# Attention scores of a perceiver block: 12 block-diagonal matmuls become 48 matmuls on 32x32 pieces of the array

## The reference

```python
q = (query @ Wq).reshape(B, L, H, D).transpose(0, 2, 1, 3)   # B=128, L=32, H=16, D=32
k = (key @ Wk).reshape(B, S, H, D).transpose(0, 2, 1, 3)     # S=257
v = (value @ Wv).reshape(B, S, H, D).transpose(0, 2, 1, 3)
attn = jnp.einsum('bhld,bhsd->bhls', q * SCALE, k)
attn = jax.nn.softmax(attn, axis=-1)
x = jnp.einsum('bhls,bhsd->bhld', attn, v)
x = x.transpose(0, 2, 1, 3).reshape(B, L, C)
return x @ Wo + bo
```

## Time and profile before

| | |
|---|---|
| median of 3 runs | 2917.51 us (2917.2 to 2921.46) |
| profiled execution, its span (the page gives no other time of it) | 2917.1 us |
| cross-attention within the span | about 126 to 1912 us |
| mean granted TensorE clock over the span | 0.980 |

### The profile page before, as it was taken

How to read it: one execution, slowest core, us unless ns; L and a number is a source line. 1 busy time by engine, 2 the same in 40 slices (tenths; PEclk the granted TensorE clock), 3 DMA queues, 4 the chain that set the end, 5 groups by cost and what they waited for, 6 DMA issues and landing times. The chain is left out here.

```text
span 2917.1 us, 54809 instructions
## 1 busy us (share of the span) xinstructions
PE 2794.1 (96%) x18492; PEld 1704.0 (58%) x18492; DVE 1668.3 (57%) x3620; ACT 1267.4 (43%) x2954; POOL 776.4 (27%) x1530
## 2 busy tenths in 40 slices
PE   7999999999999999999999999957999999899999
PEld 4455555555555555555555555534666666566666
DVE  7555555555555555555555555556665666656664
ACT  4344444444444444444444444423433443344444
POOL 2233333333333333333333333211111111111110
PEclk9999999999999999999999999978999999999999
DMA  4211111111111111111111111022000000000000
GB/s 143 83 56 55 62 41 40 40 48 41 40 40 48 41 40 40 48 41 40 40 48 41 40 40 48 13 84 66 15 30 15 15 14 22 22 14 14 14 23 15
DMA packets 65959, 118.49 MB, mean 41 GB/s; under 512 B 12016, under 2 KB 32496, under 8 KB 65392
## 3 DMA queue, kind: packets, MB, share of 16 engines
q1 hardware_dynamic: 65904, 117.76, 12.4%
HBM read 109.06 MB, written 8.65 MB: 40 GB/s over the span
## 5 line engine op out<-in xcount | busy, mean ns | idle before, releaser
L656 DVE SCALAR_TENSOR_TENSOR kT_lo<-psum,kT_hi 128x512 f16<-128x512 f32 x256 | 177.1, 692 | 440.2 <-ACT kT_hi L587 440.2
L591 ACT ACTIVATE v_hi<-psum 128x512 f16<-128x512 f32 x256 | 152.8, 597 | 552.7 <-PE psum L746 552.7
L746 PE MATMUL psum<-c_hi,xWk_hi 128*128 128x512 f16 x1024 | 388.1, 379 | 2.3 <-PEq L136 2.3
L746 PE MATMUL psum<-xWv_hi,c_hi 128*128 128x512 f16 x1024 | 388.3, 379 | 0.0
L746 PE MATMUL psum<-xWv_lo,c_hi 128*128 128x512 f16 x1024 | 388.1, 379 | 0.0
L746 PE MATMUL psum<-xWv_hi,c_lo 128*128 128x512 f16 x1024 | 388.1, 379 | 0.0
L746 PE MATMUL psum<-c_lo,xWk_hi 128*128 128x512 f16 x1024 | 388.1, 379 | 0.0
L746 PE MATMUL psum<-c_hi,xWk_lo 128*128 128x512 f16 x1024 | 388.1, 379 | 0.0
L118 POOL TENSOR_TENSOR c_lo<-ctx_raw,c_hi 128x1024 f16<-128x1024 f32 x128 | 272.5, 2129 | 429.8 <-ACT c_hi L583 419.2
L662 DVE SCALAR_TENSOR_TENSOR v_lo<-psum,v_hi 128x512 f16<-128x512 f32 x256 | 177.1, 692 | 360.4 <-ACT v_hi L591 360.4
L597 ACT ACTIVATE e<-psum,neg_max 128x257 f32<-128x257 f32 x512 | 236.3, 474 | 281.9 <-DVE neg_max L651 281.9
(11 more groups left out here) (195 smaller groups left out, 5986.9 us busy)
## 6 DMA issues: line engine op xcount, KB each, us to landing
ctx_raw<-in_ctx_main SPq DMA_DIRECT2D x128, 512.0 KB, 3.3
xs<-in_x SPq DMA_DIRECT2D x8, 1024.0 KB, 5.5
v_rep<-v_last_rows SPq DMA_DIRECT2D x512, 16.0 KB, 2.3
xb<-in_x SPq DMA_DIRECT2D x16, 512.0 KB, 3.3
out<-res_out SPq DMA_DIRECT2D x32, 256.0 KB, 2.0
ffn_raw<-in_w_t SPq DMA_DIRECT2D x11, 512.0 KB, 3.4
late_raw<-in_late_w SPq DMA_DIRECT2D x4, 1024.0 KB, 4.7
res<-in_w_t SPq DMA_DIRECT2D x5, 512.0 KB, 3.5
```

Source lines behind the costliest of these rows:

```text
L591: nc.scalar.mul(v_hi[u][:, t, :], v_bank(t), W_UNSCALE).then_inc(v_hi_done, 1)
L656: nc.vector.scalar_tensor_tensor(out=kT_lo[r][:, m, :, 0:S], in0=k_bank(m), scalar=W_UNSCALE, in1=kT_hi[r][:, m, :, 0:S], op0=ALU.mult, op ...
L746: mm = nc.tensor.matmul(bank, a, b, start=(n == 0), stop=(n == len(steps) - 1))
```

## The change

The block-diagonal tiles go. GpSimd makes two plain copies of the sample's queries, `qb_hi` and `qb_lo`, and clears nothing. TensorE multiplies each head by itself: 32 partitions of queries (32 columns of weights) by 32 partitions of keys (257 columns), with the rows of the array chosen by h and its columns by g. Sixteen heads and three passes make 48 matmuls; in a run of sixteen no two use the same 32x32 part of the array, and the four of a turn differ in both h and g. The scores of head (h, g) now lie in bank h on the partitions of g, where before they lay in bank g on the partitions of h. What follows is adapted to that: the outputs of bank h read the values of its four heads as four runs of 32 columns, the replicated last values are cut the other way, the last values are stored unpermuted, and the output weight's rows are loaded in the new order by four transfers; the three other late weights come by four transfers each as well. The first quad of SyncE is written out ahead of its loop. The waits in front of the scores move ahead of the last value matmul of the step before.

```diff
+                for qb, heads in ((qb_hi, heads_hi), (qb_lo, heads_lo)):
+                    nc.gpsimd.tensor_copy(qb[:, :, :], heads[:, :, bass.ds(b * L, L)]).then_inc(qb_ready, 1)
...
+                for n, (a, w) in enumerate(steps):
+                    if scores_next and n == len(steps) - 1:
+                        await_scores(*scores_next)
+                    mm = nc.tensor.matmul(v_bank(t), a, w, start=(n == 0), stop=(n == len(steps) - 1))
...
-                for g in range(KC):
-                    mm = run(psum[:, g, 0:S + 1],
-                             [(q[:, g, :, :].rearrange("p h l -> p (h l)"), k[u // 2][:, g, u % 2, 0:S + 1])
-                              for q, k in passes(bd_hi, bd_lo, kT_hi, kT_lo)])
+            def score(i, u):
+                for n, (q, k) in enumerate(passes(qb_hi, qb_lo, kT_hi, kT_lo)):
+                    for turn in range(KC):
+                        for h in range(HPG):
+                            g = (h + turn) % KC
+                            rows, outs = slice(32 * h, 32 * h + 32), slice(32 * g, 32 * g + 32)
+                            mm = nc.tensor.matmul(psum[outs, h, 0:S + 1], q[rows, g, :],
+                                                  k[u // 2][rows, g, u % 2, 0:S + 1], start=(n == 0),
+                                                  stop=(n == 2))
                 mm.then_inc(s_ps, 1)
...
+                for h in range(HPG):
+                    cols = slice(h * P, (h + 1) * P)
+                    mm = run(out_bank[:, h, :],
+                             [(p[:, t, cols], v[:, t, :].rearrange("p (g h d) -> p h g d", g=KC, h=HPG)[:, h])
...
+                for g in range(KC):
+                    rows = slice(32 * g, 32 * g + 32)
+                    sp.dma_start(late_raw[rows, :, :], late_w[bass.ds(n, 1), rows].rearrange("o p n -> p o n")
+                                 ).then_inc(late_landed, 16)
```

More of the change, by code:

```diff
@@ L492, in load_last, with load_output_weight @@
                 past(sp, last_done, b - 1)
[L493 to L495 removed]
+                for g in range(KC):
+                    sp.dma_start(v_rep[u % 2][g * L:(g + 1) * L, :, :].rearrange("p h d -> p (h d)"),
+                                 v_last_rows[bass.ds(b, 1), g * P:(g + 1) * P].to_broadcast([L, P])
                                  ).then_inc(rep_landed[u % 2], 16)
+            def load_output_weight():
+                by_slot = late_w[0:1].rearrange("o (h d) (g n) -> g d (o h) n", h=HPG, g=KC)
+                for g in range(KC):
+                    sp.dma_start(late_raw[32 * g:32 * g + 32, 0, :].rearrange("p (h n) -> p h n", h=HPG),
+                                 by_slot[g]).then_inc(late_landed, 16)
             def load_late(n):
                 past(sp, late_lo_done, KC * n)
[L500 to L501 removed]
+                for g in range(KC):
+                    rows = slice(32 * g, 32 * g + 32)
+                    sp.dma_start(late_raw[rows, :, :], late_w[bass.ds(n, 1), rows].rearrange("o p n -> p o n")
+                                 ).then_inc(late_landed, 16)
             def quad(i, late=False, end=False):
@@ L513, in _ @@
                 load_last(b, b)
-            with sp.Fori(0, LATE) as i:
+            load_output_weight()
+            quad(0)
+            with sp.Fori(1, LATE) as i:
                 quad(i, late=True)
@@ L549, in last_token @@
                 b = i * 4 + u
-                pool.wait_ge(bd_ready, 2 * HPG * (b + 2 if more else b + 1))
+                pool.wait_ge(qb_ready, 2 * (b + 2 if more else b + 1))
                 pool.wait_ge(e_done, KC * (b + 1))
@@ L754, in keys, with values, await_scores @@
                                 for w, c in passes(wk_hi, wk_lo, c_hi[r], c_lo[r])]).then_inc(k_ps, 1)
-            def values(b, u, t):
+            def values(b, u, t, scores_next=None):
                 past(pe, v_lo_done, ST * (b - 1) + t + 1)
                 rows = slice(t * P, (t + 1) * P)
[L759 to L763, removed]
+                steps = [(c[:, k, u % 2, rows], w[:, k, :]) for k in range(KC)
+                         for c, w in passes(c_hi[u // 2], c_lo[u // 2], wv_hi, wv_lo)]
+                for n, (a, w) in enumerate(steps):
+                    if scores_next and n == len(steps) - 1:
+                        await_scores(*scores_next)
+                    mm = nc.tensor.matmul(v_bank(t), a, w, start=(n == 0), stop=(n == len(steps) - 1))
+                mm.then_inc(v_ps, 1)
+            def await_scores(i, u):
                 b = i * 4 + u
-                pe.wait_ge(bd_ready, 2 * HPG * (b + 1))
+                pe.wait_ge(qb_ready, 2 * (b + 1))
                 pe.wait_ge(k_col, 2 * (i * 2 + u // 2 + 1))
@@ L786, in outputs @@
                 pe.wait_ge(v_lo_done, ST * (b + 1))
[L787 to L790, removed]
+                for h in range(HPG):
+                    cols = slice(h * P, (h + 1) * P)
+                    mm = run(out_bank[:, h, :],
+                             [(p[:, t, cols], v[:, t, :].rearrange("p (g h d) -> p h g d", g=KC, h=HPG)[:, h])
+                              for t in range(ST)
+                              for p, v in passes(pT_hi, pT_lo, v_hi[u % 2], v_lo[u % 2])])
                 mm.then_inc(pv_ps, 1)
@@ L805, in step @@
                 if more:
-                    values(b + 1, (u + 1) % 4, 1)
+                    values(b + 1, (u + 1) % 4, 1, (i + u // 3, (u + 1) % 4))
             for m in range(KC):
@@ L810, in _ @@
             values(0, 0, 0)
-            values(0, 0, 1)
+            values(0, 0, 1, (0, 0))
             with pe.Fori(0, QUADS - 1) as i:
```

25 lines of the change are left out of this document (7 added, 18 removed).

## The result

The changed kernel takes 2847.93 us (median of 4 runs, 2846.59 to 2849.26) against 2918.82 us (2917.2 to 2921.46, 4 runs) for the kernel before: a ratio of 0.9756, with a 95% interval of 0.9743 to 0.9770, or 70.9 us less.

The account below looks back on a forecast made before the run. TensorE, busy 96% of the span, was taken to bound the kernel; scores of 0.72 + 0.11 + 0.16 = 0.99 us in place of 1.32 save 0.33 us in 126 steps: 2917.5 - 41.6 = 2876 us, range 2820 to 2968.

Parts of the forecast that it names:

- The 48 starts: Scores on TensorE: 48 weight loads one behind another at 15 ns, 0.72 us a step.
- the first rival: Scores: all sixteen pieces stream together, nothing drains, sequencer sets the pace; 0.57 us a step, 2824 us; chance 0.21.
- The sequencer's pace: TensorE's sequencer hands out score pairs at 10 ns each, 0.46 us for 48; a lower bound on the starts.
- The seams: Entry to and exit from the score pieces: 0 to 0.16 us each; one tail of 0.16 us taken.
- the tail of 0.16: A whole-array matmul's record outlasts its slot by 0.16 us, lost at a seam if the array must run empty.
- The slower rivals: Scores: pieces cost the array more than their share; slower had 0.31 in all, 2967 us at 30 ns a pair.
- 30 ns a pair: Scores: each pair takes 0.03 us, place 1.71 us, 2967 us; within the 0.22 for 22 to 35 ns or rows in turn.
- 56 ns a pair: Scores: a new load waits for the running piece, place 2.96 us, 3124 us; chance of no overlap 0.07.
- rows that take turns: Scores: four pieces of a row take turns, twelve turns of 0.11 us; 2958 us with both tails, 2917 with none.
- Cover: Transposes behind the scores wait for no exponential: 1.42 us spare in regular steps, 0.71 in sixteen late-weight steps; steps 126, 127 wait.
- The terms at zero: Moved waits, GpSimd's copies, outputs with broken-up values and SyncE's extra transfers: cost or gain 0 each.
- The moved waits: Five waits one value matmul earlier, 0.22 us: 0.9 us covers it, VectorE's sums come last; cost 0.

Follow-up runs that it names:

- the run with two more changes: Changed kernel with the first two score passes ahead of the last value matmul and the third behind it: 2871.96 us, ratio 0.9842 to the kernel before.
- the run with rows in turn: Changed kernel with the four score pieces of one array row directly behind one another, then the next row: 2849.83 us.
- the head-by-head order: Changed kernel with the three score passes of one head directly behind one another on the same piece, then the next head: 2904.7 us.
- in the outputs: Changed kernel with each of the 24 output matmuls cut into four of 128x32 on column strips, 96 in all: 2798.22 us, ratio 0.9582 to the kernel before.
- the run with two passes: Changed kernel without the third score pass (low half of the queries by high half of the keys), 32 pairs in place of 48: 2822.03 us.
- with half the columns: Changed kernel with each score piece streaming only the first 128 of 257 columns of keys: 2837.05 us.

## Why the prediction came out as it did

**What bounds the kernel: right.** TensorE's busy time and the step shrank together, at a mean granted clock of 1.00 in the stage before and after, and nothing took its place. TensorE's waits between 130 and 1830 us are two of 1.6 us, against 2.6 us in all in the earlier trace rows:

```profile
PE psum L791 <- ACT e L597: 1.6, 1, 1.6
PE psum L746 <- DVE pT_lo L669: 1.6, 1, 1.6
```

**The 48 starts: the term that was mis-sized.** 0.72 us forecast, 0.43 measured; these 0.29 us times 126 are 36.5 us, against the 31 us by which the cross-attention's 72.7 us exceed the forecast 41.6 (the seams give the rest back). The step that failed is the choice of the earlier trace rows as the price. Those two loads, 15 ns apart, fill the whole array, and the trace of before does not show them as the prediction read them, with no stream between: the first one's matmul starts 4 ns behind its load and 11 ns ahead of the second load, and the granted clock there (1899.95 to 1900.05 us) is 0.50.

```profile
1899.99 0.29 PE L746 MATMUL psum<-v_hi,pT_hi 128*128 128x128 f16 x1 [1.56 <-DVE pT_lo L669]
```

Loads into different pieces start 3.3 ns apart. The Trainium skill, TensorE: Matmul & The Clock Gate, section Measured speedup vs the span model, has about 4 ns from tile to tile; the 3.3 ns of the first two passes agree, the 8.3 ns of the third do not. I named that figure in the prediction and put it with the rival.

**The sequencer's pace** of 10 ns a pair, worked out from the earlier trace rows, was the better guide: 8.3 ns measured, but for the third pass alone, since some 32 pairs already stand queued while the value matmul ahead of them streams. The rival that used it (0.46 us of starts) was near for the starts, and wrong about the seams. Its 2824 us were missed by 24 us, the forecast's 2876 by 28.

**The seams: right in kind.** Neither is free: 0.093 us on entry, 0.102 + 0.01 on exit, 0.20 together where I took 0.16 of 0 to 0.32. Both cost, and each less than the tail of 0.16. In the run with two more changes they cost 0.094 to 0.105 us again. The Trainium skill, TensorEngine Tiling (Array Packing), section Key Properties, has a change of tiling mode drain TensorE; a cost of about 0.1 us at every change agrees. Whether the array runs quite empty isn't shown, since the ends of matmuls are modelled (the last value matmul's record of 0.38 us outlasts the first piece's start at 0.31). The rule in its section Instruction Overhead, 60 cycles for each matmul, does not hold between pieces: 3.3 and 8.3 ns from start to start, where 60 cycles at 2.4 GHz would be 25 (an estimate from that page). It does show between matmuls on the same strip: 25 to 28 ns for 32 columns.

**The slower rivals fell.** 30 ns a pair, 56 ns a pair and rows that take turns are all refuted by the starts (the last also by the run with rows in turn). A distance of about 25 ns does occur, but for another reason: in the head-by-head order it is three pairs, and in the outputs it is the same strip used again.

**Cover: right.** A regular step (ScalarE's last sum, then the transposes, as in the earlier trace rows):

```profile
1013.62 0.21 ACT L597 ACTIVATION_READ_ACCUMULATOR e<-psum,neg_max 128x1 f32 x1
1014.73 1.04 PE L791 MATMUL psum<-ident,e 128*128 128x128 f32 x8
```

leaves 1014.73 - (1013.62 + 0.21) = 0.90 us, 0.52 less than in the earlier trace rows; a late-weight step, as in the earlier trace rows,

```profile
215.27 0.21 ACT L597 ACTIVATION_READ_ACCUMULATOR e<-psum,neg_max 128x1 f32 x1
215.73 1.04 PE L791 MATMUL psum<-ident,e 128*128 128x128 f32 x8
```

0.25 us, where 0.71 - 0.58 = 0.13 was to be expected. Had the scores shrunk by the 0.75 us of the first rival, the sixteen steps would have been bound by the exponentials, as the run with two passes shows at 0.85. Steps 126 and 127 wait, as forecast; what step 126 gained came from its clock, not from the scores.

**The terms at zero: right.** Outputs with values in four runs of 32 columns still start 56 ns apart:

```profile
1004.87 0.22 PE L746 MATMUL psum<-v_hi,pT_hi 128*128 128x128 f16 x1
1004.93 0.22 PE L746 MATMUL psum<-v_lo,pT_hi 128*128 128x128 f16 x1
```

GpSimd's two copies are 0.59 us a step, just under the 0.6 to 0.8 taken from the earlier trace rows (the page's groups: busy us, mean ns of one, idle before and its releaser):

```profile
L540 POOL COPY qb_lo<-heads_lo 128x128 f16 (+1 forms) x128 | 37.9, 296 | 0.0
```

and eight copies take the same time for the whole kernel. The moved waits have their 0.8 to 0.9 us of cover. No wait of TensorE leads back to SyncE's additional transfers.

## What to carry to other kernels

When a matmul uses only blocks of the array, cut it into pieces that share no part of it and put a whole round of different pieces ahead of the second use of any. In these runs pieces then cost their streams and hardly their number, up to some 32 pairs, and beyond that the 8.3 ns at which the sequencer hands out each pair. Count about 0.1 us for each change between whole array and pieces, and so put all the pieces of a step in one place. Before you price a new small instruction by a row, ask whether the row's instructions share the resource that the new ones don't: two loads into the whole array do not price loads into different parts of it. Look, too, at what the row's view leaves out: here the granted clock, and the matmul between the two loads.

## What the runs showed of the hardware

- Pieces start 3.3 ns apart when they stand queued and 8.3 ns apart when the queue is used up; about 32 to 33 pairs are in flight, and the next comes 27 to 28 ns after the first of these records ends (306 after 279 ns; 253 after 225; 216 after 189 in the outputs).
- Pairs for different pieces pass one another: with the passes of a head in a row, starts came in three rounds of eleven heads, and the 48 starts took 846 ns in place of 430. Room for new pairs came free in program order all the same (417 ns, 28 behind the second pair's end; 527 ns, 28 behind the third's).
- The same piece starts again 14 ns after its stream (121 after 107 ns; 67 after 53 ns); the same strip of 32 columns with 32 columns streamed after 25 to 28 ns, of 64 with 64 after 31.4 ns.
- A change between whole array and pieces cost 0.09 to 0.11 us, behind streams of 257 columns (scores) and of 32 (outputs, whose last start was 117 ns ahead of the next value matmul); with half the columns the change back took up to 0.16 us.
